# A ring of six units of states, sums two places later in TensorE's order, gates in the third unit

## What is computed

```python
x_ssm = silu(causal_conv4(h @ Win[:, :512]) + conv_b)
z = h @ Win[:, 512:]
dt = softplus(x_ssm @ dt_w + dt_b)
A = -exp(A_log)
Bt, Ct = x_ssm @ Bp, x_ssm @ Cp
def step(state, inp):                    # for each token
    dA = exp(dt_t[:, :, None] * A[None])
    state = state * dA + (dt_t * x_t)[:, :, None] * B_t[:, None, :]
    y_t = einsum('bds,bs->bd', state, C_t)
y = (ys + x_ssm * D) * silu(z)
return x + y @ Wout
```

## Time and profile before

| what | value |
|---|---|
| median of 3 runs | 5458.74 us (5453.97 to 5460.18) |
| the profiled execution | 5458.95 us |
| its span | 5457.0 us |
| PE busy | 4824.3 us, 88% |
| DVE busy | 4908.5 us, 90% |
| ACT busy | 3914.1 us, 72% |
| POOL busy | 5026.0 us, 92% |
| PE's granted clock, mean | 0.98 of 2.4 GHz |
| moved by DMA | 976 MB, 179 GB/s |

### The profile page before, as it was taken

How to read it: one execution, slowest core, us unless ns; L and a number is a source line. 1 busy time by engine, 2 the same in 40 slices (tenths; PEclk the granted TensorE clock), 3 DMA queues, 4 the chain that set the end, 5 groups by cost and what they waited for, 6 DMA issues and landing times.

```text
span 5457.0 us, 189369 instructions
## 1 busy us (share of the span) xinstructions
PE 4824.3 (88%) x85070; PEld 2954.7 (54%) x85070; DVE 4908.5 (90%) x4595; ACT 3914.1 (72%) x6659; POOL 5026.0 (92%) x2310
## 2 busy tenths in 40 slices
PE   4798989989898998989989898998989989899887
PEld 2455555555555555555555555555555555555554
DVE  1699989999999999999999999999999999999997
ACT  3776777767778676777767778676777767766564
POOL 0699899999999999999999999999999999999997
PEclk8899999999999999999999999999999999999999
DMA  5565565656556565565656556565565656556553
GB/s 168 153 170 184 170 185 184 178 188 170 192 177 181 188 176 196 169 190 180 181 186 173 194 176 182 185 177 189 171 190 183 177 190 172 186 176 174 191 181 121
DMA packets 578860, 976.04 MB, mean 179 GB/s; under 512 B 294881, under 2 KB 328450, under 8 KB 510466
## 3 DMA queue, kind: packets, MB, share of 16 engines
q1 hardware_dynamic: 313858, 961.82, 55.3%
q10 hardware_dynamic: 264192, 2.11, 2.8%
HBM read 875.74 MB, written 88.08 MB: 177 GB/s over the span
## 4 chain that ended last, share of the span: by engine, by line
POOL 45%; PE 36%; DVE 9%; issue 8%; ACT 1%; DMA 0%; ACTq 0%; DVEq 0%; POOLq 0%
POOL H L661 41%; PE Y L748 13%; PE pUB L724 12%; DVE H L603 8%; PE pP L682 5%; PE pP L688 3%; PE pA L768 2%; POOL dto L642 1%; POOL duo L648 1%; POOL lnv L637 1%; DVE cv L554 1%; PE Y L737 0%; PE pA L762 0%; DVE X L558 0%; DMA Cb<-scratch_c 0%
## 5 line engine op out<-in xcount | busy, mean ns | idle before, releaser
L661 POOL TENSOR_TENSOR H<-H,Cb 128x1024 f32<-128x1024 f32 x2048 | 4788.9, 2376 | 235.7 <-DVE H L603 218.2
L603 DVE TENSOR_TENSOR_SCAN H<-dA,pUB 128x512 f32<-128x512 f32 x4096 | 4671.1, 1200 | 362.7 <-PE pUB L724 345.3
L440 ACT ACTIVATE dA<-DT,w_negA 128x512 f32<-128x512 f32 x4096 | 2620.1, 711 | 1325.8 <-DVE H L603 1319.8
L724 PEld LDWEIGHTS pUB<-Bd,UT 64*64 64x64 f32 x65536 | 1896.6, 134 | 1343.1 <-issue 882.2
L724 PE MATMUL pUB<-Bd,UT 64*64 64x128 f32 x65536 | 2225.3, 273 | 390.8 <-DVE H L603 378.7
L748 PE MATMUL Y<-H,w_ident 64*64 64x512 f32 x16384 | 1990.6, 599 | 120.7 <-POOL H L661 119.4
L748 PEld LDWEIGHTS Y<-H,w_ident 64*64 64x64 f32 x16384 | 609.9, 134 | 735.0 <-issue 541.8
L682 PE MATMUL pP<-hT,w_Win 128*128 128x512 f32 x512 | 272.4, 657 | 15.2 <-DVE cv L554 12.1
L688 PE MATMUL pP<-U,w_dt_w 128*128 128x512 f32 x512 | 257.2, 627 | 6.6 <-DVE ev L617 4.8
L440 ACT ACT_TABLE_LOAD x178 | 228.4, 1283 | 3.2
L554 DVE SCALAR_TENSOR_TENSOR cv<-pP,w_conv_w,cv 128x511 f32<-128x511 f32 (+2 forms) x192 | 139.0, 724 | 33.9 <-ACT cv L378 33.6
(11 more groups left out here) (80 smaller groups left out, 1706.0 us busy)
## 6 DMA issues: line engine op xcount, KB each, us to landing
Cb<-scratch_c SPq DMA_DIRECT2D x512, 1024.0 KB, 5.2
Bd<-scratch_diag SPq DMA_DIRECT2D x512, 512.0 KB, 4.2
scratch_diag<-H SPq DMA_DIRECT2D x16, 1024.0 KB, 16.9
scratch_z<-zo SPq DMA_DIRECT2D x64, 256.0 KB, 6.1
scratch_dt<-dto SPq DMA_DIRECT2D x64, 256.0 KB, 7.7
scratch_ut<-uto SPq DMA_DIRECT2D x64, 256.0 KB, 7.3
DT<-scratch_dt SPq DMA_DIRECT2D x64, 256.0 KB, 5.2
UT<-scratch_ut SPq DMA_DIRECT2D x64, 256.0 KB, 5.9
```

The costliest lines, as they stand in the source:

```text
L440: last = nc.scalar.activation(dA[:, n % DAR, j, :], DT[:, k, :], ACT.Exp, scale=c["negA"][:, k, GS * blk + j:GS * blk + j + 1])
L603: last = nc.vector.tensor_tensor_scan(H[:, n % HR, 2 * i + j, :], dA[:, n % DAR, 2 * i + j, :], pUB[:, i, :].rearrange("p (t s) -> p s t", ...
L661: nc.gpsimd.tensor_tensor(h[:, j:j + 2, :], h[:, j:j + 2, :], Cb[:, blk % 2, j:j + 2, :], ALU.mult).then_inc(times_c, 1)
L724: last = nc.tensor.matmul(out, UT[rows, k, j * P + h * HP:j * P + h * HP + HP], Bd[rows, blk % 2, i, j * P:(j + 1) * P].rearrange("p (t s) ...
```

## The change

HR, the units in the ring H, goes from 4 to 6, and a unit's slot is its number over all batches modulo 6 instead of its place modulo 4, since 64 is no multiple of 6. In PE's order each half of a pair's sum moves two places later: at an even n it is now half 1 of the pair n-4, which waits for POOL's second half of unit n-3, and at an odd n half 0 of the pair n-3, which waits for POOL's first half of unit n-2; the last pairs of a batch are summed in places 0, 1 and 2 of the next. The two skip_over stand right ahead of the first sum of their half batch, so in places 3 and 35. The gates move from ahead of unit 2 to behind the first scan of unit 3, and from ahead of unit 34 to behind the first scan of unit 35. For room in SBUF two tiles go: a row of `norms` becomes the small tile `rs_more`, and `ev1` is written over `absv`. No instruction is added or removed.

```diff
--- before.py
+++ after.py
@@ -17,7 +17,7 @@
-DAR, HR = 2, 4
+DAR, HR = 2, 6
...
-    norms = sb("norms", [P, 4, 6, NJ])
+    norms, rs_more = sb("norms", [P, 4, 5, NJ]), sb("rs_more", [P, NJ])
...
-    absv, lnv, ev1, relu = (sb(n, [P, T]) for n in ("absv", "lnv", "ev1", "relu"))
+    absv, lnv, relu = (sb(n, [P, T]) for n in ("absv", "lnv", "relu"))
...
-            def between(b, n, i, close, proj, ffn):
+            def between(b, n, i, scan, close, proj, ffn):
 
                 c_, q, a = b - 1, b + 1, b + 2
                 when = DVES
+                if close and n == 3 and i == 0:
+                    gate(c_, 2)
+                    gate(c_, 3)
+                if scan and n == HALF + 3 and i == 0:
+                    gate(b, 0)
+                    gate(b, 1)
                 if proj and n in when["conv"] and i:
                     m = when["conv"].index(n)
                     convolve(KI * q + m, m, i)
@@ -584,12 +590,6 @@
                 c_, q, a = b - 1, b + 1, b + 2
                 when = DVES
                 for n in range(GN):
-                    if close and n == 2:
-                        gate(c_, 2)
-                        gate(c_, 3)
-                    if scan and n == HALF + 2:
-                        gate(b, 0)
-                        gate(b, 1)
                     if scan:
                         u = GN * b + n
                         for i in range(2):
@@ -600,21 +600,21 @@
                                 dve.wait_ge(summed, at(u + 1 - HR))
                             dve.wait_ge(forced, at(2 * u + i + 1))
                             for j in range(2):
-                                last = nc.vector.tensor_tensor_scan(H[:, n % HR, 2 * i + j, :], dA[:, n % DAR, 2 * i + j, :],
+                                last = nc.vector.tensor_tensor_scan(H[:, u % HR, 2 * i + j, :], dA[:, n % DAR, 2 * i + j, :],
                                                                     pUB[:, i, :].rearrange("p (t s) -> p s t", s=2)[:, j, :], 0.0,
                                                                     ALU.mult, ALU.add)
                                 if j:
                                     last.then_inc(state_done, 1)
-                                between(b, n, 2 * i + j, close, proj, ffn)
+                                between(b, n, 2 * i + j, scan, close, proj, ffn)
                     else:
                         for i in range(4):
-                            between(b, n, i, close, proj, ffn)
+                            between(b, n, i, scan, close, proj, ffn)
                     if close and n in when["norm c"]:
                         invert(nc, dve, rootc, flipc, normc[2], normc[3], c_)
                     if proj and n in when["soft"]:
                         m = KI * q + when["soft"].index(n)
                         dve.wait_ge(one_done, at(m + 1))
-                        nc.vector.scalar_tensor_tensor(out=ev1[:, :], in0=pP[:, :], scalar=-1.0, in1=absv[:, :],
+                        nc.vector.scalar_tensor_tensor(out=absv[:, :], in0=pP[:, :], scalar=-1.0, in1=absv[:, :],
                                                        op0=ALU.add, op1=ALU.subtract).then_inc(soft1, 1)
                     if ffn and n in when["norm 1"]:
                         invert(nc, dve, root1, flip1, norm1[2], norm1[3], a)
...
-                    nc.gpsimd.tensor_tensor(lnv[:, :], lnv[:, :], ev1[:, :], ALU.subtract).then_inc(soft2, 1)
+                    nc.gpsimd.tensor_tensor(lnv[:, :], lnv[:, :], absv[:, :], ALU.subtract).then_inc(soft2, 1)
...
@@ -651,7 +651,7 @@
                 c_, q, a = b - 1, b + 1, b + 2
                 when, turns = POOLS, DVES
                 for n in range(GN):
-                    blk, h = n % HALF // 2, H[:, n % HR]
+                    blk, h = n % HALF // 2, H[:, (GN * b + n) % HR]
                     if scan:
                         if n % 2 == 0:
                             pool.wait_ge(c_in[blk % 2], at(16 * (b * NBLK + n // 4 + 1)))
@@ -745,7 +745,7 @@
                     for r in range(2):
                         rows = slice(r * HP, r * HP + HP)
                         for i in range(2):
-                            last = nc.tensor.matmul(Y[r][i * HP:i * HP + HP, :], c["ident"][rows, rows], H[rows, (n + i) % HR, j, :],
+                            last = nc.tensor.matmul(Y[r][i * HP:i * HP + HP, :], c["ident"][rows, rows], H[rows, (GN * b + n + i) % HR, j, :],
                                                     start=False, stop=(n % HALF == HALF - 2 and j == GS - 1))
                 if half:
                     last.then_inc(summed, 2)
@@ -840,6 +840,17 @@
                         pe.wait_ge(h_out, at(2 * a + i))
                         transpose(i, t2)
 
+            def sum_states(b, n, scan, close):
+
+                p, half = (n - 4, 1) if n % 2 == 0 else (n - 3, 0)
+                if scan and p >= 0:
+                    if p % HALF == 0 and half == 0:
+                        skip_over(b, p)
+                        skip_over(b, p + 1)
+                    add_states(b, p, half)
+                if close and p < 0:
+                    add_states(b - 1, GN + p, half)
+
             def step(b, scan, close, proj, ffn):
                 for n in range(GN):
                     if scan and n + 1 < GN:
@@ -848,21 +859,16 @@
                         force(b + 1, 0, 0)
                     if n % 2:
                         other(b, n, close, proj, ffn)
-                    if scan and n % 2 == 0 and n:
-                        add_states(b, n - 2, 1)
-                    if close and n == 0:
-                        add_states(b - 1, GN - 2, 1)
+                    if n % 2 == 0:
+                        sum_states(b, n, scan, close)
                     if scan and n + 1 < GN:
                         force(b, n + 1, 1)
                     if proj and n + 1 == GN:
                         force(b + 1, 0, 1)
                     if n % 2 == 0:
                         other(b, n, close, proj, ffn)
-                    if scan and n % HALF == 1:
-                        skip_over(b, n - 1)
-                        skip_over(b, n)
-                    if scan and n % 2:
-                        add_states(b, n - 1, 0)
+                    if n % 2:
+                        sum_states(b, n, scan, close)
 
             steps(pe, step)
 
```

More of the change, by code:

```diff
@@ L228, in layers @@
     junk = sb("junk", [P, NJ, DM], mybir.dt.bfloat16)
-    norms = sb("norms", [P, 4, 6, NJ])
-    norm1, norm2, norm3, normc = ([norms[:, i, what, :] for what in range(6)] for i in range(4))
+    norms, rs_more = sb("norms", [P, 4, 5, NJ]), sb("rs_more", [P, NJ])
+    norm1, norm2, norm3, normc = ([norms[:, i, what, :] for what in range(5)] for i in range(4))
     hT, U = sb("hT", [P, KM, T]), sb("U", [P, KI, T])
@@ L512, in step @@
                         normalize(nc, act, flip2, X1, XA, norm2[3], norm2[4], n2, a)
-                        nc.scalar.activation(norm2[5], norm2[3], ACT.Copy, bias=1.0).then_inc(rs_one, 1)
+                        nc.scalar.activation(rs_more[:, :], norm2[3], ACT.Copy, bias=1.0).then_inc(rs_one, 1)
                     if ffn and n == when["norm 2"][4]:
@@ L517, in step @@
                         for j in range(NJ):
-                            last = nc.scalar.activation(X1[:, j, :], X1[:, j, :], ACT.Identity, scale=norm2[5][:, j:j + 1], bias=norm2[4][:, j:j + 1])
+                            last = nc.scalar.activation(X1[:, j, :], X1[:, j, :], ACT.Identity, scale=rs_more[:, j:j + 1], bias=norm2[4][:, j:j + 1])
                         last.then_inc(r_done, 1)
```

## The result

The changed kernel takes 5431.61 us (median of 6 runs, 5417.95 to 5435.33), the kernel before 5455.81 us (median of 6, 5451.28 to 5460.18). The ratio is 0.9951 [0.9938, 0.9963]: faster, by 24 us, where 64 were forecast. The profiled execution of after took 5432.28 us around a span of 5430.4.

What follows compares the result with a forecast made beforehand. The prediction took POOL as the bound, through its idle time mostly in units 0 to 29. Its terms, -64 - 12 - 1.5 + 13.5 = -64 us, gave 5395 us, with a range of 5338 to 5432 us.

Steps and rivals of the forecast that it cites:

- what bounds the kernel: Whole batch: POOL is the slower engine, working 314.13 of 327.68 us; its idle 13.55 us is the most to win.
- the carry: Across the batch's end: later sums let POOL carry more backlog, limited by Bd's landing; 4.6 us a batch, 64 us.
- Rival (a): Bd at the batch's start does not bind, so lag grows to its natural 12 us: 5344 us, chance 0.30.
- The skip: skip_over in places 3 and 35: its eight matmuls cost 0.9 us in each of 15 batches, +13.5 us.
- the last batch: Last batch, without projections: of the 1.7 us that POOL stands, 1.5 us would go.
- Units 30 to 63: POOL's idle time there, 15.1 us over 15 batches: 12 us taken as gone, between 0 and 15.
- Gates in unit 3: Gates moved behind unit 3's first scan: DVE pays the same 1.18 us and nothing queued behind loses; no cost.
- Rival (c): Units 50 to 63: PE's waits for Bd halve its clock, nothing is saved, skip's cost remains: 5472 us, chance 0.05.
- Where ACT came in: ACT's silu at unit 5 waits for the later skip, with a dA of 2.6 us ahead of it: nothing.

Runs made afterwards that it cites:

- bd_late_units: Changed kernel with Bd loaded one pair of units sooner, only for units 40 to 63 and 2 to 5, no idle matmuls; 5460.27 us, ratio 0.9962 to before.
- bd_late_units_busy: Changed kernel with four idle matmuls and Bd loaded one pair sooner, only for units 40 to 63 and 2 to 5; 5420.47 us, ratio 0.9893 to before.
- bd_ahead_busy: Changed kernel with four idle matmuls and Bd loaded one pair of units sooner everywhere, ahead of the wait for Cb's buffer; 5486.91 us, ratio 1.0021.
- after_again: The changed kernel with no edit, run again on another chip; 5444.09 us, ratio 0.9952 to the kernel before.
- no_skip: Changed kernel without the matmuls of skip_over, so the term x D is left out of the output; 5430.25 us, ratio 0.9913 to before.
- pe_kept_busy: Changed kernel plus four idle matmuls behind place 2 of PE's order in batches 1 to 14; 5408.72 us, ratio 0.9869 to before.
- kept_busy_again: Repeat on another chip of the changed kernel with four idle matmuls behind PE's place 2; 5417.99 us, ratio 0.9886 to before.
- before_busy: Kernel before plus six idle matmuls ahead of the half sum in place 49; 5471.05 us, ratio 1.0000 to the kernel before.
- gates_second_half: Changed kernel with the gates behind the third scan of units 3 and 35 instead of the first; 5417.71 us, ratio 0.9886 to before.
- x_behind_bd: Changed kernel with the load of X of unit 0 issued behind Bd instead of ahead of it; 5450.06 us, ratio 0.9949 to before.

## Why the prediction was wrong, step by step

**Right: what bounds the kernel, and the carry.** POOL, and only its idle time in units 0 to 29 counts: the change of POOL's idle time (26.6 us) is the change of the span. PE no longer waits for POOL at unit 51 and DVE has no gap of 4.6 us there (one of 1.7 in the mean at unit 52 is new, behind Bd; it is gone in bd_late_units and bd_late_units_busy, which load Bd sooner there). The next bound is Bd behind Cb and X: it lands in 5.8 us at the median, 7.6 at the start of batch 6. 4.6 us a batch against POOL comes close to what is seen in the kernels in which the clock at unit 3 doesn't eat it: 142.4 and 142.5 us idle where 137 were worked out. Rival (a), natural lag of 12 us and 5344 us, is out by the landings, and bd_ahead_busy shows that lag of 12 us can be had but not for nothing.

**The smaller terms.** The skip came out right, 0.8 to 0.9 us a batch by the traces (0.9 forecast), and the last batch, 1.7 us (1.5 forecast). Units 30 to 63 gained 9.3 us where 12 were forecast, but this stretch varies by as much from one run of a kernel to the next, and in after_again it has 16.2 us idle, no less than before. So the fit of the 9.3 may be luck; this term is neither borne out nor refuted.

**Wrong: "Gates in unit 3. [...] Nothing to nothing."** The step looked at what DVE's gates wait for, and at what they cost DVE, and both are nothing more than before. It did not ask who waits for the scan behind them. PE does: the first forcing of unit 4 needs that scan, and PE had stood 1.86 us there already. That made 3.06 us, TensorE went to 1.2 GHz, the z projection took 1.65 us longer in batch 6 and 1.2 us in the mean, and it lies between DVE's two forcings of unit 4. Where the step had nothing, DVE's gap in unit 4 grew by 1.5 us a batch, +21 us, and more hangs on it. Rival (c) had this very mechanism, a stand of about 3.2 us and half the clock behind it, but put it at Bd's landing in units 50 to 63 at a chance of 0.05. It came true at another place and with another cause: neither Bd nor POOL made the stand long, DVE's own order did. Its own place shows the mechanism too: in after PE stood 2.9 to 3.6 us for Bd at unit 52 or 58 in six of batches 1 to 14, and in five of them the clock went to 1.2 GHz during the stand or within 1.2 us behind it. But POOL is idle for only 5.8 us in units 30 to 63 of all batches, so these stands cost at most some of the lag carried out of their batch (7.4 us at unit 63 of batch 4, 10.0 at most elsewhere).

**Size of it.** Of the 36 us missing in units 0 to 29, keeping PE busy brings back 31.0 and moving the gates 26.5, each alone. The slow projection and the slow forcing around it, by DVE's gap in unit 4 (1.62 less 0.09, 14 times), are 21 of them. A further part is at unit 15. There PE stands 1.86 us ahead of a z projection too, and the clock behind it fell in batches 0, 1, 9 and 13 of before, but in ten of after. Batch 5 and batch 6 of after, the projection and then DVE's first gap behind it:

```profile
1910.06 1.98 PE L682 MATMUL pP<-hT,w_Win 128*128 128x512 f32 x4
...
1915.83 2.33 DVE L603 TENSOR_TENSOR_SCAN H<-dA,pUB 128x512 f32<-128x512 f32 x2 [0.29 <-PE pUB L724]
```

```profile
2234.85 3.68 PE L682 MATMUL pP<-hT,w_Win 128*128 128x512 f32 x4
...
2239.63 2.33 DVE L603 TENSOR_TENSOR_SCAN H<-dA,pUB 128x512 f32<-128x512 f32 x2 [1.52 <-PE pUB L724]
```

1.52 less 0.29 is 1.2 us in such a batch; over batches 1 to 14 DVE's mean gap in unit 16 went from 0.32 to 0.94 us, which is 9 us. Why the clock falls there more often stays open. That it does so because it fell at unit 3 is not what the traces show: in no_skip it fell at unit 3 in all 14 batches and at unit 15 in one, in pe_kept_busy and kept_busy_again at unit 3 in none and at unit 15 in five and six. The 6 us that are left of the 36 are then in the carried backlog, as an estimate: 189.0 us, plus 21.4, 12.9 and 8.7 for DVE's longer gaps in units 4, 5 and 16, less 173.4, is 58.6 us, 4.2 a batch where 4.6 were forecast.

**Where ACT came in.** Its silu waited 35.6 us in all for the later skip, in the page's group of that table load. The prediction had "nothing", and DVE's waits for dA did not grow (7.3 us in all, 9.4 before), so no gap seems to follow from it; this is read from the traces only.

## What to carry to other kernels

When an operation is moved within an engine's order, ask who waits for the instruction right behind it, and read how long that engine stands there already: a stand that grows from 1.9 to 3.1 us can cost, behind its own length, up to twice the time of the next matmuls. Carried backlog is worth only what the stretch up to where it is spent lets through, so each gap between the place where it is won and the place where it pays has to be looked at under the new order. If TensorE has to stand ahead of work on the critical path, put the other engine's extras where TensorE has work, and fill the rest of the stand with matmuls of no use; in the one place tried where another engine was the bound they gained nothing.

## What the hardware showed beside this

- Four idle matmuls, 1.99 us of TensorE in each of 14 batches, made the kernel faster by 0.7 to 0.8%.
- A stand of 1.86 us at the same place was followed by 1.2 GHz in one of 14 batches of the kernel before, in 4 of before_busy and in 7 of gates_second_half; one of 3.06 us in all 14, in each of five profiles (after, after_again, no_skip, x_behind_bd, bd_late_units), on all three chips of the experiments. The stand's length alone doesn't decide: elsewhere stands of 3.24 us (after, batch 5, unit 52) and of 3.40 and 3.29 us (gates_second_half, batches 5 and 10) were followed by 2.4 GHz.
- The same 512 KB load landed in 4.2 us at the median when it was issued 3.9 us behind the load of 1 MB (median of before), and in 5.8 us at 2.6 us behind it (after); 0.85 us behind it and with another 512 KB between them it took 7.6.
- The kernel before ran at 5455.8 us in the case's runs and at 5473 to 5479 us on the three chips of the experiments, the changed one at 5431.6 and 5444.1, with ratios that agree to 0.0001. For one kernel with idle matmuls the ratios on two chips were 0.0017 apart.
